# Recall stage: the 27 placing operations of the edge search, one to a step of the last two pairs

## The reference, cut to what matters

```python
    sim = jnp.einsum('bihd,bjhd->bhij', q, k)
    sim = jnp.where(causal, sim, neg)
    attn = jax.nn.softmax(sim, axis=-1)
    out = jnp.einsum('bhij,bjhd->bhid', attn, v)
    return out.transpose(0, 2, 1, 3).reshape(b, n, HEADS * DIM) @ Wo
```

```python
    src = jnp.concatenate([edge_index[0], loops])
    dst = jnp.concatenate([edge_index[1], loops])
    e = jax.nn.leaky_relu(a_src[src] + a_dst[dst], negative_slope=0.2)
    denom = jax.ops.segment_sum(jnp.exp(e - e_max[dst]), dst, num_segments=M)
```

## Time and profile before

| | us |
|---|---|
| median of three runs | 5440.1 |
| the runs | 5429.24, 5440.1, 5451.2 |
| the profiled execution | 5436.34 |
| its span, first to last instruction | 5434.7 |
| recall stage: first Vector instruction to the histogram's copy | 2971.39 to 3844.12 |
| next stage's first Vector instruction | 3847.82 |

### The profile page before, as it was taken

How to read it: one execution, slowest core, us unless ns; L and a number is a source line. 1 busy time by engine, 2 the same in 40 slices (tenths; PEclk the granted TensorE clock), 3 DMA queues, 4 the chain that set the end, 5 groups by cost and what they waited for, 6 DMA issues and landing times. The chain is left out here.

```text
span 5434.7 us, 70881 instructions
## 1 busy us (share of the span) xinstructions
PE 4514.4 (83%) x24566; PEld 2740.3 (50%) x24566; DVE 3523.1 (65%) x8760; ACT 2183.2 (40%) x3715; POOL 937.3 (17%) x1106
## 2 busy tenths in 40 slices
PE   7797899999999999999998899999489999961004
PEld 3463344444444444444554555555379899861002
DVE  7546677777777776777654677777455555774325
ACT  1352344444444444444443445444334444320001
POOL 0122111111111111111000000000033320005771
PEclk9555899999999999999999899999589999985556
DMA  2004354666454546564553401110110010000110
GB/s 69 8 1 100 98 139 126 144 118 144 119 139 117 136 119 131 120 136 119 136 135 105 120 25 36 34 26 1 24 25 15 7 20 6 7 2 7 20 14 12
DMA packets 324643, 389.21 MB, mean 72 GB/s; under 512 B 119857, under 2 KB 274749, under 8 KB 323492
## 3 DMA queue, kind: packets, MB, share of 16 engines
q1 hardware_dynamic: 233848, 185.45, 17.0%
q0 software_dynamic: 58368, 172.46, 10.4%
q10 hardware_dynamic: 32076, 26.80, 2.7%
HBM read 313.90 MB, written 70.64 MB: 71 GB/s over the span
## 5 line engine op out<-in xcount | busy, mean ns | idle before, releaser
L1072 PE MATMUL mem_kv<-mem_weights,mem_table 128*128 128x456 f32 x4608 | 1955.7, 546 | 0.0
L1340 DVE SCALAR_TENSOR_TENSOR mem_weights<-mem_above,mem_exps 128x912 f32<-128x912 f32 x1152 | 1272.7, 1105 | 685.5 <-ACT mem_exps L1217 682.5
L1217 ACT ACTIVATE mem_exps<-mem_above 128x912 f32<-128x912 f32 x1152 | 1069.7, 929 | 931.5 <-PE mem_above L1059 931.3
L1072 PEld LDWEIGHTS mem_kv<-mem_weights,mem_table 128*128 128x128 f32 x4608 | 871.5, 189 | 566.9 <-issue 451.0
L1059 PE MATMUL mem_above<-mem_operands,mem_selector 123*128 123x456 bf16 x2304 | 636.6, 357 | 57.8 <-DMA mem_inv_z<-scratch_inv_z 32.5
L2195 DVE TENSOR_REDUCE mha_chunk_max<-mha_max_scores 114x1 f32<-114x342 f32 x864 | 438.5, 513 | 326.4 <-PE mha_max_scores L2063 311.6
L2086 PE MATMUL mha_sums<-mha_probs,mha_value_wide 114*72 114x114 f32 (+1 forms) x5184 | 607.2, 261 | 14.2 <-ACT mha_probs L2177 14.2
L2086 PEld LDWEIGHTS mha_sums<-mha_probs,mha_value_wide 114*72 114x72 f32 (+1 forms) x5184 | 559.4, 143 | 23.3 <-issue 21.3
L1059 PEld LDWEIGHTS mem_above<-mem_operands,mem_selector 123*128 123x128 bf16 x2304 | 218.2, 98 | 574.9 <-issue 462.6
L2177 ACT ACTIVATE mha_probs<-mha_scores 114x912 f32<-114x912 f32 x324 | 297.5, 930 | 377.8 <-PE mha_scores L2075 377.8
L960 POOL DMA_DIRECT2D mem_table<-in_L_ffn_tables_dram x288 | 153.3, 538 | 1365.0 <-PE mem_kv L1072 1359.7
(11 more groups left out here) (591 smaller groups left out, 5257.6 us busy)
## 6 DMA issues: line engine op xcount, KB each, us to landing
mem_table<-in_L_ffn_tables_dram POOLq DMA_DIRECT2D x288, 512.0 KB, 6.0
mem_operands<-scratch_second_scores SPq DMA_DIRECT2D x216, 256.5 KB
mem_operands<-scratch_first_scores SPq DMA_DIRECT2D x288, 128.2 KB
mem_inv_z<-scratch_inv_z SPq DMA_DIRECT2D x72, 228.0 KB
scratch_second_scores<-mem_sel_parts ACTq DMA_DIRECT2D x81, 171.0 KB
scratch_first_scores<-mem_sel_parts ACTq DMA_DIRECT2D x108, 114.0 KB
scratch_mem_q<-mem_weights SPq DMA_DIRECT2D x16, 513.0 KB, 6.0
scratch_mem_keys<-mem_kvT SPq DMA_DIRECT2D x72, 114.0 KB, 9.5
```

The source lines that it names most:

```text
L1072: last = nc.tensor.matmul(acc[k][:, 0:SPAN], table[:, k, ch, :], W[:, J % 3, c, :], start=(ch == 0), stop=(ch == CHUNKS - 1))
L1217: nc.scalar.activation(E[:, J % 2, :, :], psD[J % 2][:, :, 0:SPAN], ACT.Exp).then_inc(exped, 1)
L1340: nc.vector.scalar_tensor_tensor(W[:, J % 3, :, :], psD[J % 2][:, :, 0:SPAN], 0.0, E[:, J % 2, :, :], ALU.is_ge, ALU.mult).then_inc(weight ...
```

## The change

`place` becomes a generator, defined ahead of the loop. Its operations, their order and their operands are the same; a `yield` stands behind each linked operation (the memset goes with the one that follows it), and the wait for the end of the search moves in with it. The loop over the steps asks for one operation at the end of each step of the pairs from `PLACE_FROM` on, and what is left, if anything, is run behind the loop.

```diff
+        PLACE_FROM = 2 * FIRST_ROUNDS // len(SEARCH_AT)
...
+            def place():
+
+                V = nc.vector
+                st = Steps(dve, splaced)
+                dve.wait_ge(eiota, 5)
+                dve.wait_ge(estep, FIRST_ROUNDS * EXTRACT_STEPS)
+                L = edge.found[:, 0:FIRST]
...
+                st.link(V.tensor_scalar(valid, L, -SHIFT - 1.0, None, ALU.is_gt))
+                yield
+                st.link(V.tensor_scalar(t, L, -SHIFT, None, ALU.max))
+                yield
...
+                st.mark(V.memset(same[:, 0:1], 0.0))
+                st.link(V.tensor_tensor(same[:, 1:FIRST], r[:, 1:FIRST], r[:, 0:FIRST - 1], ALU.is_equal))
+                yield
...
+                st.link(V.tensor_tensor(over, over, t, ALU.add))
+                yield
+
+            placing = place()
             nc.vector.memset(edge.late[:, ECOLS + FIRST:LATE], SENTINEL).then_inc(init, 1)
...
                     if step % NF in HOT_AT:
                         one_hots(p * len(HOT_AT) + HOT_AT.index(step % NF))
-
-            def place():
...
-            dve.wait_ge(estep, FIRST_ROUNDS * EXTRACT_STEPS)
-            place()
+                    if p >= PLACE_FROM:
+                        next(placing, None)
+
+            for _ in placing:
+                pass
             dve.wait_ge(added, PAIRS * 6)
             dve.wait_ge(h_added, PAIRS * 3)
             nc.vector.tensor_copy(hsum[:, :, :], hflat[:, :].rearrange("p (t b) -> p b t", b=2)).then_inc(h_out, 1)
```

More of the change, by code:

```diff
@@ L1732, in one_hots @@
                                             ALU.is_equal).then_inc(hot, 1)
+            def place():
[4 more added lines that the diff above has]
+                L = edge.found[:, 0:FIRST]
+                valid, t, r, rem, same, k, ok = (ew[:, n, :] for n in range(7))
+                per = float(UNITS * NODES)
+                st.link(V.tensor_scalar(valid, L, -SHIFT - 1.0, None, ALU.is_gt))
+                yield
+                st.link(V.tensor_scalar(t, L, -SHIFT, None, ALU.max))
+                yield
+                st.link(V.tensor_scalar(r, t, 1.0 / per, SHIFT / per - 0.5, ALU.mult, ALU.add))
+                yield
+                st.link(V.tensor_scalar(r, r, MAGIC, MAGIC, ALU.add, ALU.subtract))
+                yield
+                st.link(V.tensor_scalar(rem, r, per, SHIFT, ALU.mult, ALU.subtract))
+                yield
+                st.link(V.tensor_tensor(rem, t, rem, ALU.subtract))
+                yield
+                st.link(V.tensor_scalar(t, rem, 0.0, None, ALU.is_lt))
+                yield
+                st.link(V.tensor_tensor(r, r, t, ALU.subtract))
+                yield
+                st.link(V.scalar_tensor_tensor(rem, t, per, rem, ALU.mult, ALU.add))
+                yield
+                st.link(V.tensor_scalar(t, rem, per, None, ALU.is_ge))
+                yield
+                st.link(V.tensor_tensor(r, r, t, ALU.add))
+                yield
+                st.mark(V.memset(same[:, 0:1], 0.0))
+                st.link(V.tensor_tensor(same[:, 1:FIRST], r[:, 1:FIRST], r[:, 0:FIRST - 1], ALU.is_equal))
+                yield
+                st.link(V.scalar_tensor_tensor(same, same, -1.0, eoff[:, 1, :], ALU.add, ALU.mult))
+                yield
+                st.link(V.tensor_scalar(same, same, -1.0, None, ALU.mult))
+                yield
+                st.link(V.tensor_tensor_scan(t, same, same, 0.0, ALU.max, ALU.max))
+                yield
+                st.link(V.tensor_tensor(k, eoff[:, 1, :], t, ALU.subtract))
+                yield
+                st.link(V.tensor_scalar(ok, k, float(CELL), None, ALU.is_lt))
+                yield
+                st.link(V.tensor_tensor(ok, ok, valid, ALU.mult))
+                yield
+                st.link(V.tensor_scalar(k, k, ew[:, 7, 0:1], None, ALU.add))
+                yield
+                st.link(V.scalar_tensor_tensor(k, r, float(128 * CELL), k, ALU.mult, ALU.add))
+                yield
+                st.link(V.tensor_tensor(k, k, eoff[:, 0, :], ALU.subtract))
+                yield
+                st.link(V.tensor_tensor(k, k, ok, ALU.mult))
+                yield
+                st.link(V.tensor_tensor(edge.place[:, :], k, eoff[:, 0, :], ALU.add))
+                yield
+                over = edge.late[:, ECOLS:ECOLS + FIRST]
+                st.link(V.tensor_tensor(t, valid, ok, ALU.subtract))
+                yield
+                st.link(V.tensor_tensor(over, L, t, ALU.mult))
+                yield
+                st.link(V.tensor_scalar(t, t, -SENTINEL, SENTINEL, ALU.mult, ALU.add))
+                yield
+                st.link(V.tensor_tensor(over, over, t, ALU.add))
+                yield
```

## The result

The changed kernel takes 5430.5 us in the median, against 5442.0 us for the kernel before on the same chips: a ratio of 0.9978 with a 95% interval of 0.9970 to 0.9985, or 8 to 16 us less. The profiled execution has a span of 5424.9 us, 9.8 us under that of before. Forecast were 5431.0 us and a gain of 9.1 us, as 0.17%. One of the 22 runs of the changed kernel took 5874.5 us, at a granted clock of 0.777 against 0.879 to 0.882 in the others; the ratio leaves it out.

A forecast was written before the change was run, and what follows sets the result against it. TensorE was taken to bound the pairs' steps, the Vector engine alone (place) the stage's end. Median 5440.1 us less 9.1 at the end, plus 0 in the steps, gave 5431.0 us, range 5416 to 5446.

The forecast's parts named there:

- The end of the stage: Behind the last add of the recall stage: without place there, the histogram's copy starts 9.1 us earlier.
- The bound of 1.3 us for the closing: End of the recall stage: if closing needed the memory stage's 4.77 us, 1.3 us of gain lost, 7.8 left.
- The steps at 0: Steps of pairs 14 and 15: the moved operations fit the Vector engine's idle times and cost 0 us.
- the 0.6 us allowed: Steps of pairs 14 and 15: upper bound on their cost, for two late operations at 0.3 us.
- those that I had listed as tight: Steps 13 to 15 and 17 of pair 14, 1 to 5 of pair 15; add of step 6 0.3 us late, PE unaffected.
- The strongest argument for 0: Pair 13, step 3: a MAX8 of 2.29 us made tile 7's maximum 1.23 us late, tile 8's not at all.
- The clock: Rival, TensorE's low-clock stretch in pair 14 or the last pair changes: 5437.6 or 5424.4 us; chance 0.04 each way.
- The price I gave to the rival, 6.6 us: Clock rival: 13 us more or less at half the clock, half of it loss, is 6.6 us; chance 0.04 each way.
- The range: Whole kernel: 5416 to 5446 us, from 11 us run spread and the clock's 6.6 us, plus the medians' uncertainty.
- the rule's price on GpSimd: Last pairs: by the shared-port rule one GpSimd sum may be held by up to 0.3 us, forecast total unchanged.

The follow-up runs named there:

- e4_behind: Kernel before, with the 27 operations in one piece behind the histogram's copy instead of ahead of it; 5436.5 us against 5435.8, ratio 0.9998.
- e5_skip: Changed kernel, but no placed operation in steps 1, 2, 3 and 4; 5422.0 us against 5429.7 of the kernel before, ratio 0.9981.
- e2_twice: Changed kernel with the whole placing issued twice, two operations to a step; 5420.5 us against 5435.8 of the kernel before, ratio 0.9975.
- f2_shift: Kernel before, but two placing operations between the two maxima of tile 8 in pair 15; low stretch 17.1 us, tail 22.68 us, no total time given.
- f4_shift: Kernel before, but four placing operations between the two maxima of tile 8 in pair 15; low stretch 6.8 us, tail 17.82 us, no total time given.
- e8_late: Changed kernel, histogram's copy between the last adds, two operations between tile 8's maxima in pair 15; 5418.7 us against 5437.6 of the kernel before, ratio 0.9966.
- e3_lump: Changed kernel, but all 27 operations in one lump at the end of step 9 of pair 15; 5425.0 us against 5435.8 of the kernel before, ratio 0.9977.

## Why the prediction was right, and where it was not

**The end of the stage** was right in each step: 0.34 us for an operation, 0.03 us from the last `add` to the copy, 9.09 us in all, and a tail of 3.70 us behind the copy that stays. The bound of 1.3 us for the closing, taken from the end of the memory stage, was not needed: e4_behind shows the closing alone to take 1.17 us, with 2.3 us of store ahead of it.

**The steps at 0** were mis-sized: they cost 0.56 us, inside the 0.6 us allowed, but at other places than those I had listed as tight. I had followed the lateness to the `add` of step 6 of pair 15, which tile 8 waits for. Against PE that `add` is 0.06 us late and not 0.3: it ends at 3798.23, and PE's product starts 0.62 us later, where it was 0.68 before. I had not followed the operation of step 1. The `add` of step 2 stands right behind it, and PE's second projection waits for that `add`. In the changed kernel, pair 15:

```profile
3787.16 0.29 DVE L1783 SCALAR_TENSOR_TENSOR rec_edge_work<-rec_edge_work 128x168 f32<-128x168 f32 x1
...
3787.48 0.67 DVE L1710 SCALAR_TENSOR_TENSOR hidden<-rec_ninth,rec_inv_sums,hidden 114x64 f32<-114x64 f32 x3
...
3788.25 0.78 PE L1586 MATMUL rec_ninth<-rec_wo,rec_outT 64*114 64x64 f32 x6 [0.16 <-issue]
```

Against the kernel before, PE's instructions are shifted by 0.24 us more behind this projection than ahead of it, and by 0.12 us (PE's own spacing, some of it given back) at the same place in pair 14. e5_skip takes both away. The rest, some 0.25 us, is 0.05 to 0.07 us wherever a maximum is the first work behind a placed operation, even where the Vector engine had been idle for 2 us in between; at tile 8, at whose maxima PE's restart hangs, PE is late by it. The placed operation adds a wait for `splaced` to those that stand ahead of the maximum, and the program has 9 instructions more than before; whether the extra wait is what delays the start was not tried.

**The strongest argument for 0**, the MAX8 of pair 13, was sound for what it covers, Vector lateness of 1.23 us at tile 7: in e2_twice, with more lateness than that, 0.99 us are lost at tile 8 of pair 14, which fits. It says nothing of the `add` of step 2, since the MAX8 stands in step 3.

**The clock** is the step that failed. I had it as a rival of 0.04 each way and as luck, on the ground that PE is not moved. PE was moved, by 0.5 us against the clock's fall, and that (f2_shift moves nothing else of PE) took 3.4 us off the low stretch of the last pair and 2.2 us off the tail, in each trace alike. The forecast of 9.1 us is near the measured 10.7 us of the trace because +0.6 and -2.2 us were both missing from it and partly cancel. That the median fell within 0.5 us of the 5431.0 us is luck besides: the kernel before has moved from 5440.1 to 5442.0 us with more runs, and the spread of the runs is many times this. The price I gave to the rival, 6.6 us if the last stretch became as short as pair 14's, is what f4_shift and e8_late measured: 7.0 us. The range, made for the spread of the runs, took all of it in.

The Trainium skill, TensorE: Matmul & The Clock Gate, Part 1, says that the gate's activity window runs freely, so that a kernel may warm up at different moments in different runs. The first half fits the traces: the falls behind tile 8 stay 51.20 us apart where PE's restart moves. In the second half they differ: the tail is 24.81 to 24.84 us in the three that leave PE alone, and 22.63 to 22.64 us in the three with the changed kernel's steps, on more than one chip.

The earlier pairs show how that comes about. In pair 2 the fall comes 19.5 to 20.3 us after the inversion of step 1, at a different place from trace to trace (there are fourteen). From there to pair 10 the time from one pair's inversion to the next creeps to 51.20 us, from below (before: 51.13, 51.13, 51.17, 51.18 us) or from above (f2_shift: 51.22, 51.21, 51.21 us), while the falls behind tile 8 are 51.20 us apart (the last of e2_twice excepted), and in pair 12 the fall comes 20.24 to 20.28 us after the inversion in every one. The steps have settled against the clock's falls before the change begins, which would explain why the same program finds the same clock in its last pair again. What pulls them there was not tried.

**The shared port.** In pair 14 a one-hot that began 0.07 us after GpSimd's sum took 0.92 us, where the other one-hots take 0.69 or 0.70:

```profile
3739.32 0.43 POOL L1512 TENSOR_TENSOR rec_hist_sums<-rec_hist_sums,rec_outT 128x130 f32<-128x130 f32 x1 [7.21 <-ACT rec_outT L1654]
```

```profile
3739.39 0.92 DVE L1729 TENSOR_TENSOR rec_hist_onehot_low<-rec_hist_low,rec_iota_rows 128x1040 bf16<-128x1040 bf16 x1
```

Before, the one-hot had begun first, and the sum took 0.59 us; the earlier trace rows show the same in pair 15. The Trainium skill, SBUF — State Buffer, says that which of the two blocks is a matter of who starts first; the traces agree in which one takes longer. The prediction had put the rule's price on GpSimd, where nobody waits. Most of it fell on the Vector engine, 0.23 and 0.22 us once in each pair, at tile 7 (in pair 15 the sum took 0.52 us besides). In amount the rule is not borne out: when the one-hot began, 0.36 us of the sum were left, and it took only 0.23 us longer.

## What to carry to other kernels

A stretch at the end of a stage in which a single engine works is worth its full length, and 27 small operations fit into the gaps of a busy loop for 0.6 us here; but follow each to the next instruction of its own engine and to who reads that one, not only to the gap that looks smallest. Where the loop has a wait behind which TensorE's clock falls, compare the intervals and the low stretches of two traces before crediting an edit with its gain: here 0.5 us of delay gave back 2.2 us, and 1.1 us gave back 7.0. And a store that ends a stage should be issued when its data are ready, not when the engine's list is done: 1.7 to 2.2 us here.

## What was unexpected of the hardware

- The length of TensorE's low stretch in the last pair depends in steps on how long PE still stands after the clock's fall: 20.5 us for up to 0.6 us, 17.1 us for 0.8 to 0.9 us (in e3_lump in two pieces), 6.8 us for 1.4 us. In the windows shown of them the records have PE busy for 19.8 of 20.3, 16.2 of 17.0 and 5.3 of 6.7 us, so more idle time at their start went with an earlier return. Which property of the work does, was not tried and stays open.
- The changed kernel's steps gave the same length in three traces on more than one chip, to 0.1 us: in every trace the pairs had settled to 51.20 us, the spacing of the clock's falls, well before.
- In e2_twice the clock fell in the middle of a pair for 6.8 us, after waits of PE of 1.27 and 0.58 us. The kernel before has the first of them there too (1.21 us) and not the second, and its clock stays at 1.00.
